# Attention maxima: one 512-column chunk of 5 in 16 query blocks is copied to SBUF by ScalarE and folded by GpSimd

## The reference

```python
q = _rms_norm(q, q_norm_w); k = _rms_norm(k, k_norm_w)      # 16 heads of 8
q = _apply_rope(q, rope_cos, rope_sin); k = _apply_rope(k, rope_cos, rope_sin)
q = q / math.sqrt(HEAD_DIM)
scores = jnp.einsum('bqhd,bkhd->bhqk', q, k)
attn = jax.nn.softmax(scores.astype(jnp.float32), axis=-1)
out = jnp.einsum('bhqk,bkhd->bqhd', attn, v).reshape(b, s, HIDDEN)
```

## Time and profile before

| | |
|---|---|
| median of 3 runs | 1900.57 us (1896.1 to 1901.75) |
| the profiled execution's own time | 1906.93 us |
| its span from the first to the last instruction | 1905.1 us |
| granted clock of TensorE, mean | 0.952 |
| busy of the span | PE 94%, DVE 85%, ACT 76%, GpSimd 18% |
| attention phase, first maxima to last exps | about 395 to 1640 us |

### The profile page before, as it was taken

One profiled execution on the slowest core, in us unless ns is written; L12 is line 12 of the kernel. 1 busy time (PEld: TensorE's weight loads), 2 busy tenths in 40 slices (PEclk: granted clock), 3 DMA queues, 4 the chain that ended last, 5 costly groups with the idle time before them and its releaser, 6 DMA issues. The chain is left out here.

```text
span 1905.1 us, 37687 instructions
## 1 busy us (share of the span) xinstructions
PE 1791.9 (94%) x14923; PEld 754.7 (40%) x14923; DVE 1615.3 (85%) x1934; ACT 1454.3 (76%) x2709; POOL 344.2 (18%) x416
## 2 busy tenths in 40 slices
PE   5699997869999999999999999999999999899998
PEld 3477875711222222222222222222222223377776
DVE  6466665689999999999999999999999993377765
ACT  2355553615999999999999999999999996556554
POOL 4266660210000000000000000000000000145565
PEclk9799996857999999999999999999999998899999
DMA  4444330220010010001001001000000100433452
GB/s 116 89 121 126 118 99 1 85 98 1 20 36 22 20 31 27 20 26 33 20 21 37 20 20 35 23 20 30 28 20 26 33 28 3 87 108 113 107 138 72
DMA packets 66309, 98.81 MB, mean 52 GB/s; under 512 B 11995, under 2 KB 33312, under 8 KB 66116
## 3 DMA queue, kind: packets, MB, share of 16 engines
q1 hardware_dynamic: 61974, 94.32, 17.4%
q10 hardware_dynamic: 4160, 2.10, 0.4%
HBM read 84.94 MB, written 11.04 MB: 50 GB/s over the span
## 5 line engine op out<-in xcount | busy, mean ns | idle before, releaser
L1290 DVE TENSOR_REDUCE at_mx<-ps 128x1 f32<-128x1024 f32 x1024 | 1165.7, 1211 | 10.3 <-PE ps L1202 8.2
L1157 ACT ACTIVATE at_prob<-ps 128x512 f32<-128x512 f32 x2048 | 1097.9, 596 | 77.6 <-PE ps L1220 32.1
L1230 PE MATMUL ps<-at_prob,vals 128*32 128x256 f32 x8192 | 657.0, 392 | 13.3 <-ACT at_sums L1164 13.3
L1202 PE MATMUL ps<-k_head,q_head 48*128 48x512 bf16 x2048 | 638.9, 392 | 14.7 <-PEq L789 7.8
L1220 PE MATMUL ps<-q_head,k_head 51*128 51x512 bf16 x1924 | 584.6, 383 | 2.8 <-ACT at_prob L1157 2.8
L1230 PEld LDWEIGHTS ps<-at_prob,vals 128*32 128x32 f32 x8192 | 162.4, 108 | 429.0 <-ACT at_prob L1157 408.0
L674 POOL TENSOR_TENSOR e_part<-e_silu,e_cw 128x512 f32<-128x512 f32 (+1 forms) x208 | 268.0, 1289 | 304.8 <-DMA e_cw<-comb_rows 120.8
L688 DVE TENSOR_TENSOR ps<-e_part,ps 128x512 f32<-128x512 f32 (+1 forms) x208 | 144.7, 696 | 166.5 <-POOL e_part L674 166.2
L1220 PEld LDWEIGHTS ps<-q_head,k_head 51*128 51x128 bf16 x1924 | 117.9, 93 | 404.3 <-ACT at_prob L1157 385.1
L644 ACT ACTIVATE e_silu<-ps 128x512 f32<-128x512 f32 (+1 forms) x208 | 124.2, 597 | 158.7 <-PE ps L598 157.8
L651 ACT ACTIVATE q_head<-ps 128x512 fp32r<-128x512 f32 (+1 forms) x208 | 124.2, 597 | 49.3 <-DVE ps L688 38.2
(11 more groups left out here) (229 smaller groups left out, 1112.0 us busy)
## 6 DMA issues: line engine op xcount, KB each, us to landing
e_cw<-comb_rows SPq DMA_DIRECT2D x80, 256.0 KB, 3.3
e_cw<-comb_rows SPq DMA_DIRECT2D x32, 224.0 KB, 3.1
e_cw<-comb_rows SPq DMA_DIRECT2D x32, 192.0 KB, 3.1
q_head<-q_rows SPq DMA_DIRECT2D x64, 96.0 KB
k_head<-k_rows SPq DMA_DIRECT2D x64, 96.0 KB
e_cw<-comb_rows SPq DMA_DIRECT2D x32, 160.0 KB, 2.8
e_cw<-comb_rows SPq DMA_DIRECT2D x48, 96.0 KB, 2.6
e_cw<-comb_rows SPq DMA_DIRECT2D x32, 128.0 KB, 3.0
```

The lines of the kernel that those rows point to most:

```text
L1157: act.activation(prob[:, g % PROBS, c, :], ps[:, S + bank(i, g, c, last), :], ACT.Exp).then_inc(exped, 1)
L1202: one = pe.matmul(ps[:, at, :], q[i][HALF:HALF + KR, (j // CHUNKS) * P:(j // CHUNKS + 1) * P], k[i][HALF:HALF + KR, c * BLK:(c + 1) * BLK] ...
L1230: done_one = pe.matmul(ps[32 * j:32 * j + 32, O, half * HALF_BLK:(half + 1) * HALF_BLK], vals[i][:, g, :], prob[:, g % PROBS, 2 * half + j ...
L1290: dve.tensor_reduce(mx[i][:, j // 2, j % 2:j % 2 + 1], ps[:, at:at + 2, :].rearrange("p a t -> p (a t)"), AX.X, ALU.max).then_inc(max_redu ...
```

## The change

For five query blocks of each head, 1, 4, 7, 10 and 13 (`RELAYED`), the first pair of chunks is shared out. DVE reduces only its first bank, 512 columns. ACT copies the other bank to SBUF (`pass_on`, into `relay`, which is the `rope` tile, two buffers in turn). GpSimd halves the 512 columns five times down to 16 (`fold`), each time with three instructions, since max(a, b) = max(a - b, 0) + b: subtract, clamp at 0, add. The 16 columns of each of the five blocks wait in `folds` (`swap` and a new tile in turn), and at the head's end DVE reduces 5 x 16 columns to five maxima, which it puts in a third place of `mx`. Places that are not used hold -3.0e38. There are 160 such copies in all, 7 of them ahead of the first turn.

ACT does the copy behind the third exp of a slot: in slots 1, 4 and 7 for blocks 7, 10 and 13 of the next head, in slots 11 and 14 for blocks 1 and 4 of the one after it. Before it reuses a buffer it waits for the fold two before. PE waits with the maxima matmul that takes the copied bank's pair next, which is the first one in the slot that follows, for the copy as well as for DVE.

```diff
+    RELAYED = range(1, KT, 3)
+    FOLD, FOLDS = 16, 15
+    def relay_beside(h, g):
+        at = (h + 1, KT - LAG + g - 1) if g <= LAG else (h + AHEAD, g - LAG - 1)
+        return at if at[0] < BH and at[1] in RELAYED else None
...
+            def fold(h, u):
+                n = relay_number(h, u)
+                pool.wait_ge(relayed, n + 1)
+                if h >= 2:
+                    pool.wait_ge(max_found, h - 1)
+                at = n * FOLDS
+                m = BLK // 2
+                while m >= FOLD:
+                    low, high = relay[:, n % 2, 0:m], relay[:, n % 2, m:2 * m]
+                    if m < BLK // 2:
+                        pool.wait_ge(folded, at)
+                    pool.tensor_tensor(low, low, high, ALU.subtract).then_inc(folded, 1)
+                    pool.wait_ge(folded, at + 1)
+                    pool.tensor_scalar(low, low, 0.0, None, ALU.max).then_inc(folded, 1)
+                    pool.wait_ge(folded, at + 2)
+                    out = low if m > FOLD else fold_of(h)[:, RELAYED.index(u), :]
+                    pool.tensor_tensor(out, low, high, ALU.add).then_inc(folded, 1)
+                    at, m = at + 3, m // 2
...
+            folds_of(0, 0, NR)
+            for h in range(BH):
                 split(h, h % BUFS)
+                folds_of(h + 1, 0, 3)
+                if h and h - 1 + BUFS < BH:
                     replace(h - 1, (h - 1) % BUFS)
+                folds_of(h + 1, 3, NR)
...
+            def pass_on(h, u):
+                n, j = relay_number(h, u), 2 * u
+                act.wait_ge(max_scored, h * PAIRS_OF_HEAD + j + 1)
+                if n >= 2:
+                    act.wait_ge(folded, (n - 1) * FOLDS)
+                act.activation(relay[:, n % 2, :], ps[:, M + 2 * (j % MRING) + 1, :], ACT.Copy).then_inc(relayed, 1)
...
+                    if c == 2 and g and relay_beside(h, g):
+                        pass_on(*relay_beside(h, g))
...
                 if j % 2 == 0 and not (isinstance(n, int) and n < MRING):
                     pe.wait_ge(max_reduced, n - MRING + 1)
+                    before, u = divmod((n - MRING), PAIRS_OF_HEAD)
+                    if u % 2 == 0 and u // 2 in RELAYED:
+                        pe.wait_ge(relayed, relay_number(before, u // 2) + 1)
...
+                banks = ps[:, at, :] if j % 2 == 0 and j // 2 in RELAYED else ps[:, at:at + 2, :].rearrange("p a t -> p (a t)")
...
+                dve.wait_ge(folded, (h + 1) * NR * FOLDS)
+                dve.tensor_reduce(mx[i][:, RELAYED[0]::3, 2], fold_of(h), AX.X, ALU.max).then_inc(fold_reduced, 1)
+                dve.wait_ge(fold_reduced, h + 1 + BUFS)
```

More of the change, by code:

```diff
@@ L161, in build @@
             attention_phase(nc, sem, kept, ps, v, identb, q_head, k_head, vals, q_rows, k_rows, qk_loaded,
[L162 removed]
+                            qk_stored, sum_rows, sums_stored, late, rope, swap)
             expert_phase(nc, sem, "e3", ps, x, xnT, wgate, wup, wdown, comb_rows[1], late.comb_stored, ident,
@@ L1003, in attention_phase @@
 def attention_phase(nc, sem, kept, ps, v, identb, q, k, vals, q_rows, k_rows, qk_loaded, qk_stored,
-                    sum_rows, sums_stored, late):
+                    sum_rows, sums_stored, late, relay, even_folds):
     CHUNKS = SEQ // BLK
@@ L1023, in attention_phase @@
     TURN_MAXIMA = LAG + 3
+    RELAYED = range(1, KT, 3)
+    NR = len(RELAYED)
+    FOLD, FOLDS = 16, 15
+    LOWEST = -3.0e38
     TAIL_FROM = (BH - 2) * KT + LAG + 1
@@ L1033, in attention_phase @@
     max_found = sem("at_max_found")
+    relayed = sem("at_relayed")
+    folded = sem("at_folded")
+    fold_reduced = sem("at_fold_reduced")
     max_split = sem("at_max_split")
@@ L1041, in attention_phase, with relay_number, fold_of @@
     sums_kept = sem("at_sums_kept")
+    def relay_number(h, u):
+        return h * NR + RELAYED.index(u)
+    def relay_beside(h, g):
+        at = (h + 1, KT - LAG + g - 1) if g <= LAG else (h + AHEAD, g - LAG - 1)
+        return at if at[0] < BH and at[1] in RELAYED else None
+    def fold_of(h):
+        return folds[h % 2][:, 0:NR * FOLD].rearrange("p (r n) -> p r n", r=NR)
     def turned_at(h):
@@ L1059, in attention_phase @@
     with ExitStack() as tmp:
-        mx = [kept(f"mx{i}", [P, KT, 2]) for i in range(BUFS)]
+        mx = [kept(f"mx{i}", [P, KT, 3]) for i in range(BUFS)]
         neg = [kept(f"neg{i}", [P, KT]) for i in range(BUFS)]
@@ L1066, in attention_phase @@
         sums = kept("sums", [P, BLK])
+        folds = [even_folds, kept("odd_folds", [P, NR * FOLD])]
         prob = tmp.enter_context(nc.sbuf_tensor("at_prob", [P, PROBS, CHUNKS, BLK], F32))
@@ L1090, in split, with folds_of @@
                 pool.tensor_tensor(mparts[i][:, 2, :], res[:], mparts[i][:, 1, :], ALU.subtract).then_inc(max_split, 1)
+            def fold(h, u):
[16 more added lines that the diff above has]
+                    at, m = at + 3, m // 2
+            def folds_of(h, a, b):
+                if h < BH:
+                    for u in RELAYED[a:b]:
+                        fold(h, u)
             def replace(h, i):
@@ L1099, in _ @@
             pool.wait_ge(max_zeroed, 1)
-            for h in range(2 * BUFS):
+            folds_of(0, 0, NR)
+            for h in range(BH):
                 split(h, h % BUFS)
-                if h:
+                folds_of(h + 1, 0, 3)
+                if h and h - 1 + BUFS < BH:
                     replace(h - 1, (h - 1) % BUFS)
[L1104 to L1111, removed]
+                folds_of(h + 1, 3, NR)
         @block.sync
@@ L1185, in _ @@
             prime(act, sums_kept)
+            for u in RELAYED:
+                pass_on(0, u)
+            pass_on(1, RELAYED[0])
             keep_maxima(0, 0)
+            pass_on(1, RELAYED[1])
             exps(0, 0, 0)
@@ L1289, in reduce @@
                 at = M + 2 * (j % MRING)
-                dve.tensor_reduce(mx[i][:, j // 2, j % 2:j % 2 + 1], ps[:, at:at + 2, :].rearrange("p a t -> p (a t)"),
-                                  AX.X, ALU.max).then_inc(max_reduced, 1)
+                banks = ps[:, at, :] if j % 2 == 0 and j // 2 in RELAYED else ps[:, at:at + 2, :].rearrange("p a t -> p (a t)")
+                dve.tensor_reduce(mx[i][:, j // 2, j % 2:j % 2 + 1], banks, AX.X, ALU.max).then_inc(max_reduced, 1)
             def turn(h, i, last=False):
@@ L1304, in turn @@
                 dve.tensor_reduce(neg[i][:], mx[i][:], AX.X, ALU.max, negate=True).then_inc(max_found, 1)
+            for i in range(BUFS):
+                dve.memset(mx[i][:], LOWEST).then_inc(fold_reduced, 1)
+            dve.wait_ge(fold_reduced, BUFS)
             for j in range(2):
```

## The result

The changed kernel takes 1982.72 us, median of 4 (1974.51 to 1987.38), against 1899.99 us before (4 runs): a ratio of 1.043, 95% interval 1.039 to 1.048, slower by 4.3%. The forecast was 1959.5 us, slower. The profiled execution is the slowest of the four; it has a span of 1985.6 us, 80.5 us above the 1905.1 of before.

A forecast was written before the change was run, and what follows sets the result against it. DVE was taken to bind, 0.30 us a head ahead of PE. Stalls +70.4, DVE's bound -9.0, first turn -2.5 sum to +58.9: 1965.8 us profiled, 1959.5 median; bounds 1943 to 1973, stated range 1935 to 2000.

The forecast's parts named there:

- DVE's relief is capped by PE: Attention phase: PE's own head takes 36.15 us against 36.45, so relieving DVE gains at most 0.30 us a head.
- The stall: PE's first maxima matmul after a relay waits 0.46 us for ACT's copy, five times a head, never won back.
- the other bound of that step: PE's wake-up after the copy's end taken as 0.15 us, as for the sums, instead of 0.06: stall 0.55 us.
- GpSimd's fold: Chain of 15 GpSimd instructions for each relayed block: 6.6 us, ends 6.5 and 7.2, with 1.5 for the five clamps.
- the forecast's own head, 38.45: One head of the attention phase after the change: 36.15 + 5 x 0.46 = 38.45 us, against 36.45 before.
- the step that says GpSimd is hidden: GpSimd needs 34.5 us of a 38.4 us head, hidden by 0.8 us a fold; it binds at 7.4 us a fold.
- the 0.8 us by which the last fold was said to be covered: Head's end: the last fold ends at 8.2 us, DVE reaches its small reduction at about 9.0, so no wait.
- Rival C: The clock falls in PE's stalls; 12 us per hundredth of the phase at half clock, 2000 us and above; 4 in 100.
- Rival B: GpSimd becomes the bound, a fold over 7.4 us; with folds of 8.2 us, 2081 us in all; 10 in 100.
- rival A: The relay is hidden, PE stalls under 0.06 us and DVE's relief counts: faster, 1889 us; 7 in 100.
- -9.0 for DVE's bound: Attention phase: DVE's bound falls away, saving 0.30 us in each of 30 heads, 9.0 us in all.
- -2.5 ahead of the first turn: Before the first turn DVE paces the maxima; half reductions there save about 0.4 to 0.6 us each, 2.5 in all.

The follow-up runs named there:

- experiment 1: Changed kernel without folds, copies or the waits for them; DVE still reduces only half of the five pairs, result incomplete: 1895.19 us, ratio 0.997.
- experiment 2: Changed kernel without GpSimd's folds; ACT's copy and PE's wait for it stay, copied columns left out of the maximum: 1976.13 us, ratio 1.037.
- experiment 4: Changed kernel without folds, PE's wait for the copy moved to the second maxima matmul, which overwrites the copied bank: 1929.28 us, ratio 1.013.
- experiment 5: Kernel of experiment 2 with the two waits of PE's maxima matmul swapped, the copy asked first, then DVE's reduction: 1963.63 us, ratio 1.031.
- experiment 3: Changed kernel, complete with folds, PE's wait for the copy moved to the second maxima matmul, which overwrites the copied bank: 1979.61 us, ratio 1.040.
- experiment 10: Changed kernel with folds running on old relay contents, their result unused; no ACT copies, no PE wait for them: 1976.82 us, ratio 1.038.

## Why the prediction was right, and where it was off

*The direction and the mechanism* are shown by experiments 1, 2, 4 and 5. DVE's relief is capped by PE: 36.15 us worked out, 36.15 measured. Each relay stalls PE once and nothing wins it back: with the stalls read from single pairs, 0.53, 0.45 and 0.24, 36.15 + 5 stalls gives 38.80, 38.40 and 37.35, and the heads are 38.81, 38.42 and 37.35.

*The stall was mis-sized.* "PE starts 0.06 us after an activation that it waited for has ended" holds for a matmul with one wait, or with the late one asked first (experiment 5). The changed kernel asks for it second, and the other bound of that step, 0.15 from the sums, was the right one: 0.53 net instead of 0.46, or 153 x 0.07 = 11 us of the 22 by which the profiled execution (1987.38) came out above the 1965.8 worked out for it. The kernel had what it takes to choose between them: the weighing behind the sums asks for three semaphores with the sums' last, the scores matmul for one.

*GpSimd's fold was mis-sized, beyond its own bounds.* 6.6 us were taken, 6.5 to 7.2 given as ends; it is 7.40. The clamp was placed "nearer to the copy" and below the TENSOR_TENSOR; it is above both (0.85 us at 256 columns against 0.73). The five clamps take 2.27 us instead of 1.5, and a dependent instruction starts 0.08 to 0.09 after the one before. In the steady part this did not cost time, since the head was just long enough, 38.81 against 38.60. That it held in the forecast's terms is luck: the forecast's own head, 38.45, lies under GpSimd's 38.60. With the stall as small as forecast the folds would have set the pace, as in experiment 3, and the step that says GpSimd is hidden would have failed. But the 0.8 us by which the last fold was said to be covered had gone: the changed kernel's DVE waits 0.5 us for it in each head, which PE does not feel.

*What was overlooked* is the last head, where no reductions of a next head cover the fold. In the profiled execution it is another 10 us. Rival C, the clock falling in the stalls, was right in its kind and wrong in its place: at the 0.53 us stalls the clock stays at 1.00, behind the one of 1.58 us it falls. Rival B was nearly there, hidden 0.2 us under the stalls; rival A is refuted. The stall and the last head together account for 21 of the 22 us. The median, 1982.72, is 23 us over the forecast and lies above the forecast's own bounds, 1943 to 1973, of which the upper one is the wider stall: 1973 and the 10 us of the last head make the 1983. It lies in the stated range of 1935 to 2000 because that took in part of rival C.

*The small terms.* -9.0 for DVE's bound: experiment 1 has 1122.8 us for its 31 heads instead of 1131.3, -8.5. -2.5 ahead of the first turn: the first exp comes at 446.2 instead of 447.9, -1.7.

No complete version that was run beats the kernel before. Experiment 1, which leaves work out, shows about 0.3% (0.1 to 0.6) as all that there is to win by relieving DVE; the ways tried cost PE or DVE more than that. A version with the last chunk copied and DVE's two small reductions taken apart was not tried.

## What to carry to other kernels

Before moving work off the engine that is the bound, work out the pace of the next engine from the stretches where it catches up: here it was 1% behind, and that was all there was to win. A helper on a third engine costs by where its work is put into the order of a full one and by who waits at its end, not by its busy time alone; take the starts of the waiting instructions, and put the wait at the instruction that overwrites the buffer. And when a helper is said to be hidden, look at the margin with the error of its own sum in it: the 0.8 us a fold of the prediction were gone when the fold was measured. Two bounds can stand at one height, so undo both before saying that one is harmless, and look at the last round of a loop by itself.

## What was not expected of the hardware

- Two waits on one matmul: 0.15 us from the end of the awaited activation when the late semaphore is asked second (changed kernel, experiment 2), 0.06 when it is asked first (experiment 5) or alone (experiment 4).
- On GpSimd an fp32 clamp with one input (0.846 us at 256 columns, 0.526 at 128) is slower than a subtraction with two (0.731 and 0.457).
- GpSimd's folds beside DVE's reductions out of PSUM took nothing from them that shows: 1.22 us for 1024 columns with folds and without (changed kernel, experiment 2), 1.21 before.
- One idle time of PE of 1.58 us was followed by 20 us at a granted clock of 0.65 and 0.50; some 150 stalls of 0.53 us left it at 1.00. In between, about 1.15 us of idle time at the end of most heads (experiment 3) went with two falls of 3.4 us, and 1.7 to 2.05 us at the end of 19 heads (experiment 10) with 11 falls.
